# Column tiled value matmuls of an attention: one group for two key blocks

## What is computed

```python
logits = einsum('bhqd,bhkd->bhqk', Q, K) + b[0]      # 8 heads of 32, 2048 queries, 1601 keys
logits = logits + -1e+30 * (1.0 - mask)
weights = softmax(logits, axis=-1)
out = einsum('bhqk,bhkd->bhqd', weights, V)
```

## Time and profile before

| | us |
|---|---|
| median of 3 runs | 1328.11 (1326.83 to 1340.87) |
| the profiled execution | 1326.77 |
| its span, first to last instruction | 1325.0 |
| attention, rounds 0 to 7 | about 446 to 889 of the span |
| a round of 1 to 6 | 56.3 to 57.7 |
| mean granted PE clock | 0.938 of full |

### The profile page before, as it was taken

The page is one execution under the profiler, slowest core; times in us unless marked ns, Lnnn a source line. Parts: engine busy times, 40 slices in busy tenths (PEclk is TensorE's granted clock), DMA queues, the critical chain, the costliest instruction groups (busy, mean ns, idle before and its releaser), DMA issues.

```text
span 1325.0 us, 19280 instructions
## 1 busy us (share of the span) xinstructions
PE 1174.1 (89%) x7110; PEld 861.2 (65%) x7110; DVE 519.6 (39%) x1257; ACT 464.7 (35%) x1067; POOL 479.0 (36%) x498
## 2 busy tenths in 40 slices
PE   4767999999959899999999999999948999999985
PEld 3666999999945444444545445434448888888884
DVE  5763222211128876675767657412060000110000
ACT  4111222211100455555555565663303333333331
POOL 1241111111122475666757556660002332333331
PEclk9956999999986799999999999999958999999998
DMA  6254888888830000000000000011007999999994
GB/s 209 76 199 150 283 297 289 295 302 313 309 137 0 1 1 1 1 17 1 1 17 1 1 1 17 21 62 71 0 0 255 328 317 308 317 317 294 305 308 130
DMA packets 53977, 197.18 MB, mean 149 GB/s; under 512 B 8538, under 2 KB 34396, under 8 KB 38012
## 3 DMA queue, kind: packets, MB, share of 16 engines
q1 hardware_dynamic: 41358, 175.00, 37.3%
q0 software_dynamic: 10464, 18.36, 5.8%
q10 hardware_dynamic: 2062, 2.60, 0.6%
HBM read 179.54 MB, written 16.38 MB: 148 GB/s over the span
## 4 chain that ended last, share of the span: by engine, by line
PE 62%; DMA 20%; DVE 8%; issue 5%; ACT 2%; POOL 1%; SPq 0%; POOLq 0%; ACTq 0%
DMA out<-Z,SI 17%; PE PQ L408 14%; PE PB L513 8%; PE PB L422 7%; PE PQ L498 7%; PE PB L482 5%; PE PQ L552 4%; PE PB L286 4%; PE PB L503 4%; DVE Z L900 3%; PE PQ L482 3%; PE PB L373 2%; DMA V<-in_ctx 1%; PE PQ L286 1%; DMA Z<-xn,SI 1%
## 5 line engine op out<-in xcount | busy, mean ns | idle before, releaser
L408 PE MATMUL PQ<-Z,WS 128*128 128x128 f32 x2720 | 328.8, 277 | 12.9 <-issue 11.8
L408 PEld LDWEIGHTS PQ<-Z,WS 128*128 128x128 f32 x2720 | 323.5, 194 | 25.5 <-issue 19.2
L422 PE MATMUL PB<-WS,Z 128*128 128x256 f32 x992 | 234.3, 379 | 0.0
L900 DVE TENSOR_REDUCE Z<-PB 128x1 f32<-128x402 f32 x340 | 183.4, 567 | 88.0 <-PE PB L482 86.6
L422 PEld LDWEIGHTS PB<-WS,Z 128*128 128x128 f32 x992 | 179.1, 190 | 19.3
L498 PE MATMUL PQ<-QS,KS 128*128 128x512 f32 x416 | 173.7, 439 | 7.1 <-ACT Z L1112 4.3
L1050 ACT ACTIVATE Z<-PQ,WS 128x128 f32<-128x128 f32 x312 | 89.2, 368 | 204.6 <-PE PQ L408 182.6
L498 PEld LDWEIGHTS PQ<-QS,KS 128*128 128x128 f32 x416 | 77.6, 192 | 105.4 <-issue 60.3
L482 PE MATMUL PB<-KS,QS 128*128 128x402 f32 x340 | 133.2, 404 | 14.2 <-DVE Z L900 5.6
L1112 ACT ACTIVATE WS<-PQ 128x512 f32<-128x512 f32 x208 | 109.6, 604 | 83.5 <-PE PQ L498 83.4
L1112 ACT ACTIVATE Z<-PQ 128x512 f32<-128x512 f32 x208 | 109.5, 603 | 82.0 <-PE PQ L498 81.9
(11 more groups left out here) (240 smaller groups left out, 1207.2 us busy)
## 6 DMA issues: line engine op xcount, KB each, us to landing
WS<-in_w SPq DMA_DIRECT2D x62, 1024.0 KB, 5.1
WS<-in_w SPq DMA_DIRECT2D x23, 2048.0 KB, 8.2
WS<-in_w SPq DMA_DIRECT2D x39, 1028.0 KB
Z<-in_b SPq DMA_DIRECT2D x39, 128.0 KB
xn<-WS SPq DMA_DIRECT2D x32, 128.0 KB, 1.7
X<-in_x SPq DMA_DIRECT2D x4, 512.0 KB, 10.4
WS<-yd SPq DMA_DIRECT2D x4, 512.0 KB, 6.3
out<-X SPq DMA_DIRECT2D x4, 512.0 KB, 2.9
```

The source lines that it names most:

```text
L408: t = e.matmul(bank[:, j * P:j * P + P], w[:, k, o:o + P], FXT[i % 2][:, k * P:k * P + P], start=k == 0, stop=k == 1)
L422: t = e.matmul(y, FS[c % 4][:, j * P:j * P + P], w[:, 4 * n + j, :], start=n == 0 and j == 0, stop=n == 1 and j == 3)
L900: e.tensor_reduce(MP[j % 2][:, i:i + 1], PB[bank_of["pc", r]][:, 0:PIECE], AX.X, ALU.max).then_inc(v_pc, 1)
```

## The change

`values` takes a range of key blocks. In the step that follows an odd key block it is called with that one and the even one before it: two sets of values and, but for the first pair, one of sums in one group. Key block 12 comes alone, in step 0 of the next round, as before. So there are 7 groups a round. `val_done` follows the new order of the counts.

```diff
         def val_done(n, kc, hh):
-            before = 80 * n + 4 * kc + 4 * max(0, (kc - 1) // 2)
-            return before + hh + (5 if kc and kc % 2 == 0 else 1)
+            pair, odd = divmod(kc, 2)
+            before = 80 * n + 8 * pair + 4 * max(0, pair - 1)
+            if odd:
+                return before + 4 + hh + 1
+            return before + hh + 1 + (4 * min(2, NK - kc) if kc else 0)
...
                 if step:
                     m, j = divmod(step - 1, NK)
-                    values(m, j)
+                    if j % 2 or j == NK - 1:
+                        values(m, range(j - j % 2, j + 1))
...
-            def values(n, kc):
+            def values(n, kcs):
                 hf = n % 2
-                g = 52 * n + 4 * kc
-                e.wait_ge(a_p, g + 4)
-                if kc == 0 and n:
-                    e.wait_ge(a_ot, n)
-                for hh in range(4):
-                    e.matmul(PB[6][32 * hh:32 * hh + 32, :], V[:, kc, (4 * hf + hh) * 32:(4 * hf + hh) * 32 + 32],
-                             PT[(g + hh) % 16], start=kc == 0, stop=kc == NK - 1,
-                             tile_position=(0, 32 * hh)).then_inc(t_v, 1)
-                if not on_pool(kc):
+                for kc in kcs:
+                    g = 52 * n + 4 * kc
+                    e.wait_ge(a_p, g + 4)
+                    if kc == 0 and n:
+                        e.wait_ge(a_ot, n)
+                    for hh in range(4):
+                        e.matmul(PB[6][32 * hh:32 * hh + 32, :], V[:, kc, (4 * hf + hh) * 32:(4 * hf + hh) * 32 + 32],
+                                 PT[(g + hh) % 16], start=kc == 0, stop=kc == NK - 1,
+                                 tile_position=(0, 32 * hh)).then_inc(t_v, 1)
+                kc = kcs[0]
+                if kc:
                     if kc == 2 and n:
                         e.wait_ge(v_rt, n)
-                    summed(n, kc, kc == 2, False, lambda hh: PT[(g + hh) % 16])
+                    summed(n, kc, kc == 2, False, lambda hh: PT[(52 * n + 4 * kc + hh) % 16])
```

## The result

The changed kernel takes 1368.29 us (median of 4 runs, 1364.86 to 1370.27) against 1328.85 us (4 runs, 1326.83 to 1340.87): 1.0282 times as long, 95% interval 1.0246 to 1.0318. The sign was right, the size not: 39 us lost where 21 were expected, and the time lies outside the stated range of 1334 to 1363. The profiled execution took 1364.86 us (span 1363.0, mean granted clock 0.931).

A forecast was written before the change was run, and what follows sets the result against it. The prediction took DVE's pace, from the fifth maximum of a step on, to bound the kernel. Rounds 1 to 6 gave +16.8 us, round 0 +4, round 7 none: +21, forecast 1348 us, range 1334 to 1363.

The forecast's parts named there:

- Rival (a): PE is the bound everywhere and DVE catches up in its own gaps: 48 x 0.45 = 21.6 us faster, 1307; chance 0.08.
- The walk through the phases: Each two-step phase of a round timed from its first score: +2.1 us in rounds 1, 3, 5, +3.5 in 2, 4, 6.
- (1,2): Steps 1 and 2: one group entry and exit saved, less a loss in the transposes of the outputs, -0.3 us.
- (3,4): Steps 3 and 4: -0.4 us in odd rounds; +1.0 in even ones, where four DVE statistics stretch its pace.
- (5,6): Steps 5 and 6: DVE's split of the maxima, no longer under a group, delays the phase by +1.3 us.
- (7,8): Steps 7 and 8: eleven maxima and two early transposes, with PE behind DVE, -0.3 us.
- (9,10): Steps 9 and 10: the saving of 0.45 is eaten because DVE's lag is hidden once, +0.1 us.
- (11,12): Steps 11 and 12: PE idles until the last split, and three sets follow the transposes, +1.7 us.
- Rival (b): The losses stay small, since the split is short and transposes absorb the idle time: 1336 us; chance 0.20.
- rival (c): The clock falls after the new idle time in steps 11 and 12: seven rounds x 1.9 = 13, 1361 us; chance 0.17.
- Round 0: First round, with twelve additions on DVE: longer groups leave DVE without work; +4.5 us summed, +4 taken.
- What was costed at nothing: Step 0, round 7 (steps 4 and 5 at 6.5 us) and ACT's waits on the values: no change expected.

The follow-up runs named there:

- the last experiment: The changed kernel with the groups of round 0 left as before, one for each key block, all later rounds joined: 1361.59 us, 1.0221 times the kernel before.

## Why the prediction was right about the sign and wrong about the size

**What bounds the kernel** was right. PE busy for 95% of a round was no bound by PE; DVE's pace after the fifth maximum was (3.8 us a round come back with short reductions). Rival (a), 21.6 us faster, falls with it: L487's waits for DVE grew from 65 to 103.

**The walk through the phases** was right to 0.4 us, measured without falls of the clock:

| phase of rounds 1 to 6 | predicted | measured | by |
|---|---|---|---|
| (1,2) | -0.3 | -0.27 | 9.78 for 10.05 |
| (3,4), odd rounds | -0.4 | -0.27 | 8.24 for 8.51 |
| (3,4), even rounds | +1.0 | +1.32 | 10.36 for 9.04 |
| (5,6) | +1.3 | +1.34 | 9.11 for 7.77 |
| (7,8) | -0.3 | -0.09 | 8.51 for 8.60 |
| (9,10) | +0.1 | +0.06 | 7.82 for 7.76 |
| (11,12) | +1.7 | +1.69 | 9.02 for 7.33, the kernel without the pair over step 5 |

This gives +2.5 for an odd round and +4.1 for an even one, where +2.1 and +3.5 were predicted; over rounds 1 to 6 that is 2.7 us more than I had. Rival (b) assumed that the split is short in (5,6); it lasts 0.97 us there in the changed kernel too.

**The step that failed** is the price of the new wait in (11,12). "The phase takes 5.04 + 4.00 = 9.04 instead of 7.33: +1.7. This is the largest and the surest term" left the clock out, and put it into rival (c) with a chance of 0.17 and 1361 us, the nearest of the four figures. The wait was found as predicted, but behind it (2.02 us, where 2.5 were expected) the clock fell in all seven rounds: 10.62 + 10.66 + 10.40 + 10.61 + 10.64 + 10.73 + 10.55 less 7 x 9.02 is 11.1 us. Filling the wait took 10.4 us off the median and every fall out of (11,12), which shows the cause; a fall costs 1.64 us where (c) said 1.9, a price for which no row was given. The reason given against (c), that round 1 has pauses and clock 1.00, was no reason: the longest pause there is 1.22 us (in step 2, before 514.85), and three more are of 0.3 to 0.5. The pause in the earlier trace rows of 1.69 us with its fall in the earlier trace rows was the nearest row, and the new one is longer. One more fall came in a place that nothing in the prediction named, (3,4) of round 4, 1.4 us.

**Round 0** was expected at +4 and is +6.0, of which the fall in (11,12) is 1.6. But the kernel before has a fall in this round that the changed one lacks. The phase (5,6) of round 0, before, changed, and in the kernel with the last pair alone, in which this phase is as before:

```profile
465.32:476.26 10.94, 9.25 (x47) 4.61 (x43) 9.17 (x24) 4.28 (x8) 5.34 (x4) 0.84 0.00 1
```

```profile
470.29:481.45 11.16, 8.17 (x47) 3.83 (x43) 9.53 (x24) 4.29 (x8) 5.33 (x4) 1.00 0.00 1
```

```profile
468.14:477.57 9.43, 7.74 (x47) 3.96 (x43) 8.96 (x24) 4.13 (x8) 5.33 (x4) 1.00 0.00 1
```

At the full clock the phase is 9.43 us before and 11.16 changed, so its size is +1.7 and not the 0.2 between the first two rows, and the fall in the kernel before costs 1.5 us. The parts of round 0 without these two falls (those that both kernels have in its first steps are left in) are 1.57 before step 2's group (0.3 expected), 0.37 and 1.7 in (3,4) and (5,6) (1.2 each expected), 0.48 in (7,8) (0), 0.08 in (9,10) (0.1) and 1.7 in (11,12) (1.7): 5.9 for the 4.5 summed and the 4 taken. That 6.0 less 1.6 is near 4.5 is luck.

**The bill.** The sum of 20.8 us for the attention against 36.1 measured in rounds 0 to 7: falls 11.0 (11.1 and 1.4, less the 1.5 of the kernel before), sizes in rounds 1 to 6 2.8, round 0 1.9, round 7 -0.4; together 15.3. The other 2 us of the 38.0 are the later start (3.0) and the end (-1.1), in code that the change doesn't touch; by the runs of the last experiment such pieces differ by 3 us between executions. The remaining 3 us of the 20 between 1348 and 1368 lie in the medians, since the profiled execution of the changed kernel was its fastest, 3.4 us under its median.

**What was costed at nothing** held: step 0 is 6.76 in both; round 7 takes 46.27 for 46.66 us, its steps 4 and 5 6.50 for the 6.53 of the earlier trace rows; no wait of ACT's exponentials for PE's value or sum sets appears in the table of waits.

**What stays open**: when the clock falls. The wait before the transposes is 2.02 to 2.04 us in every kernel here that joins the last pair, leaves the wait as it is and has whole reductions. The clock fell behind it in all seven rounds of the changed kernel, in all six of the kernel with round 0 unjoined, in three of seven in the kernel with that pair alone, and in one of seven without the pair over step 5. In (3,4) of the even rounds no pause is long (0.44, 0.33, 0.33 and 0.66 us in round 2, where the clock held, and 0.44, 0.32, 0.33 and 0.65 in round 4, where it fell), and it falls in one of three rounds of the changed kernel, and in rounds 2 and 4 of the two kernels in which the wait of (11,12) is filled or the transposes come later, as in the kernel without the pair over step 5. It is so with another wait as well: in (5,6) of round 0 PE waits 1.69 us for a reduction, until 469.30 in the kernel before, where the clock fell, and until 472.11 in the kernel with the last pair alone, where it held. Where a change took falls out of (11,12), some came back elsewhere. What PE did before the wait may count, or the moment at which the wait comes; no run here tells these apart, and none moves an equal wait in time alone.

## What to carry to other kernels

A long piece of work on the faster engine isn't only a cost, it is also the time in which a slower engine that reads its results catches up; before joining such pieces, ask of each what the other engine did under it (here the splits of steps 5 and 11, and the four statistics), and join only where the answer is nothing. When a change puts a wait like this one of 2.0 us into TensorE's stream, price it twice, with and without a fall of the clock behind it, as a term and not as a remark. And look for falls in the kernel before as well, or a difference of two phases mixes the clock with the size. A PE that the profile shows busy for 95% doesn't prove that PE is the bound: the test is to make the other engine faster and see whether the round shrinks.

## What was unexpected in the hardware

**The fall of the clock comes late.** The wait of 2.02 us ended at 564.80, the clock was still 1.00 until 566.00, then 0.50; the column tiled sets, not the scores after the wait, paid for it, 1.7 us a set for 0.87.

**The same wait, with and without a fall.** With (5,6) 1.35 us shorter, the clock didn't fall behind an unchanged wait some 20 us later in six of seven rounds. It would be wrong to read this as one pause removed that protects the other: in the kernel with the last pair alone (5,6) is as short (7.76 us), and the clock fell in three of seven rounds. The Trainium skill, in TensorE: Matmul & The Clock Gate, section HAM oscillation — how this bites in real kernels, tells of kernels in which idle times between bursts bring a fall again and again; the trace agrees in (11,12), and shows besides that an equal idle time may or may not bring it.

**L888 has two durations.** The three small instructions of a split are alike in all steps, but in rounds 0 to 6 of the kernel before L888 took 0.17 us 15 times and 0.96 or 0.97 us 13 times. Its timelines of POOL and DVE in round 1 show what goes with it: at 529.88 and 554.00 (0.97 us) a chain of POOL's additions was running, at 542.56 (0.17 us) POOL's chain had ended at 541.76.

```profile
528.30 3.77 POOL L1248 TENSOR_TENSOR WS<-WS 128x512 f32<-128x512 f32 x3
...
539.23 2.53 POOL L1248 TENSOR_TENSOR WS<-WS,Z 128x512 f32<-128x512 f32 x2
```

```profile
542.56 0.17 DVE L888 TENSOR_TENSOR AU<-Z,AU 128x4 fp32r<-128x4 f32 x1
```

In the changed kernel POOL's additions lie elsewhere, and the third split of a round, short before, meets them: with a chain from 549.07 to 551.59, L895 takes 1.04 us.

```profile
549.07 2.52 POOL L1255 TENSOR_TENSOR WS<-WS,Z 128x512 f32<-128x512 f32 x2
...
550.58 1.04 DVE L895 TENSOR_TENSOR AU<-Z,AU 128x4 fp32r<-128x4 f32 x1
```

The Trainium skill says in SBUF — State Buffer, section Who interferes with whom, that a VectorE instruction with two inputs in SBUF contends with a GpSimd instruction that reads SBUF. The trace agrees: L888 has two such inputs, the reductions beside it have none from SBUF or one, and keep their 0.57 and 0.16 or 0.17 us. No run here took the additions away, so the cause is argued and not shown. By the two durations it is worth 0.8 us, an estimate, of the 1.34 us in (5,6) and of the wait of 2.0 us in (11,12).
